# One block of 128 rows in 32 is fetched row by row by SP and ACT in place of an indirect transfer

## The chip, the cores and the metric

The kernel runs on one core of a Trainium2 chip. The metric is the device time of one execution in microseconds (us). Five engines work side by side, each from its own queue: TensorE (PE), VectorE (DVE), ScalarE (ACT), GpSimd (POOL) and SyncE (SP). They wait for each other through semaphores. SP, ACT and POOL can issue DMA transfers.

## The reference

Four graph layers over 12500 nodes of 64 features and 212500 edges (src, dst), sorted by dst. Every layer begins with h = relu(layernorm(x)), and adds its result to x:

```python
h = jnp.maximum(_layernorm(x, axis=-1), 0.0)
x = x + _L0_gnn_ref(h, edge_index, edge_attr_64, ...)   # an edge MLP on h[src], h[dst] and attributes
h = jnp.maximum(_layernorm(x, axis=-1), 0.0)
x = x + _L1_gnn_ref(h, ...)                             # messages Ht[edge_type, src], summed by dst, then a GRU cell
h = jnp.maximum(_layernorm(x, axis=-1), 0.0)
x = x + _L2_gnn_ref(h, src, dst, edge_attr_8, ...)      # pair interaction on src and dst, summed by dst
h = jnp.maximum(_layernorm(x, axis=-1), 0.0)
x = x + _L3_gnn_ref(h, edge_index, ...)                 # two SAGE convolutions, each a mean of h[src] over dst
```

In three places the work on the edges is only this: fetch one row of 64 floats per edge from a table, and sum the rows by destination.

## The kernel before

The edges are cut into 416 chunks of 512 edges, a chunk into four blocks of 128. Eight chunks (RING) make a turn, so a stage has 52 turns (ITERS). The stages over the edges, in order:

- stage 0 (e = 0): the edge MLP, without gathers of rows;
- stage 1 (e = 1): plain gather from tab_msg, which has a row per node and edge type, and the GRU cell on the nodes;
- stage 2 (e = 2): gather from tab_u and the pair interaction;
- stage 3 (e = 3): plain gather from tab_h, and the first convolution on the nodes;
- stage 4 (e = 4): plain gather from tab_q, and the last sum.

In a plain stage each engine runs its own loop over turns and chunks. For chunk u of turn it:

- DVE writes the row numbers of the chunk's 512 edges into idx (L867) and a 0/1 matrix that says which node of a window of 64 each edge belongs to (L846).
- POOL waits for idx_ready and for agg_done of the same chunk of the turn before (L659 to L661; the buffers are RING = 8 chunks deep), and issues four indirect transfers, one a block (L666). Each brings 128 rows of 256 B, one into every partition, and adds 16 to gathered[u].
- PE waits until gathered[u] has the four transfers' count, and multiplies the rows by the 0/1 matrix in four matmuls with their weight loads (L1397; the trace shows eight instructions of each kind). The last adds one to agg_done.
- DVE adds the sum to acc (L836).

Nodes are dealt with in groups of 256 (49 groups) in the same loops, one group a turn, from turn WAIT_TURNS = 5 on, since by then all edges of the first group have been summed. The chain of a group in stage 1 goes back and forth: ACT copies h and the sums (L1262, L1263), PE transposes (L1500), ACT lifts (L1284), PE multiplies (L1508, L1509), ACT applies the sigmoid (L1286), DVE mixes, ACT applies tanh (L1288), DVE updates and normalises, PE transposes (L1516), ACT lifts (L1290), PE multiplies (L1521), ACT applies tanh (L1292), PE multiplies (L1527), DVE copies, and SP stores the rows in two tables (L508). PE takes its parts at fixed places among the chunks of the turn: before chunk 1, 2, 6 and 7 and after chunk 7. Stage 3 has a chain of the same kind with four steps of ACT after its copies and one store; in stage 4 it is one copy of ACT, one transpose, one step of DVE and one store.

In the plain stages ACT and SP do nothing else. Their loops run over the groups alone:

```python
            def groups(e, chain):
                with act.Fori(0, P) as p:
                    ...
                    with act.Fori(0, min(SG, whole)) as g:
                        chain(ga, turn0, g)
```

P, the number of passes over the edges, is 1 for this input. Addresses that are known only at run time go through registers: SP and DVE load the eight window starts of a turn in one instruction (L347), and a transfer or an operation then takes its address from a register.

## Time and profile before

| what | value |
|---|---|
| median of 3 runs | 10297.66 us (10293.77 to 10303.55) |
| the profiled execution | 10296.52 us, span 10294.9 us |
| busy: PE, DVE, ACT, POOL | 5755.4, 4349.8, 2458.5, 6906.9 us |
| mean granted TensorE clock | 0.687 of full speed |
| gathers (L666) | 4 x 1664, of 944 ns each (median) |
| first and last gather: stage 1, 2 | 1774.3 to 3855.9 us, 3907.6 to 6019.5 us |
| first and last gather: stage 3, 4 | 6088.1 to 8169.1 us, 8206.0 to 10281.9 us |

The span runs from the first to the last instruction of the program. Busy counts an engine's work, not its sequencer: register operations, semaphores, branches and the issue of transfers from SP and ACT are not counted as busy. PEq, SPq and the like are the sequencers.

### The profile page before, as it was taken

Reading aid. Unit: us, or ns where it says so; the run is one execution under the profiler, and the core shown is the slowest. Engines: PE = TensorE matmul, PEld = TensorE weight load, DVE = VectorE, ACT = ScalarE, POOL = GpSimd, SP = SyncE. Lnnn points to the kernel's source line nnn. Section 1 sums busy time; section 2 is a strip of 40 time slices with the busy share of each in tenths; the row PEclk is TensorE's granted clock in tenths of the full one; section 3 lists DMA queues with packets and bytes.
Section 4 is the critical chain, followed back from the end, with each engine's and each line's share of the span. In section 5 each row is a group of like instructions: output and inputs, shape, how many; then the busy total and the mean of one; then the engine's idle time right before and its main releaser. Section 6 shows DMA issues by size and latency. Waiting matters only on the chain.

```text
span 10294.9 us, 143864 instructions
## 1 busy us (share of the span) xinstructions
PE 5755.4 (56%) x32026; PEld 3571.8 (35%) x32026; DVE 4349.8 (42%) x12092; ACT 2458.5 (24%) x4667; POOL 6906.9 (67%) x7939
## 2 busy tenths in 40 slices
PE   6999996244444447999999963333333322222222
PEld 4777774222222223444444422322222211111111
DVE  6888885123232225777777751111111111111111
ACT  5999994000000002333333310000000000000000
POOL 3333332777777776777777757777777677777777
PEclk9999998555555558999999975555555555555555
DMA  3333333111111112222222211111111111111111
GB/s 105 97 96 96 97 96 123 27 30 29 30 29 30 29 29 53 61 61 62 61 60 61 61 35 27 28 28 28 28 28 28 24 27 28 28 28 28 28 28 27
DMA packets 503896, 488.63 MB, mean 47 GB/s; under 512 B 245340, under 2 KB 299425, under 8 KB 503777
## 3 DMA queue, kind: packets, MB, share of 16 engines
q0 software_dynamic: 220480, 235.58, 12.0%
q1 hardware_dynamic: 283360, 252.43, 8.5%
q8 instruction: 20, 0.33, 0.0%
q14 instruction: 36, 0.29, 0.0%
HBM read 427.04 MB, written 61.15 MB: 47 GB/s over the span
## 4 chain that ended last, share of the span: by engine, by line
POOL 46%; PE 27%; issue 18%; DVE 5%; POOLq 1%; ACT 1%; DVEq 1%; DMA 0%; SPq 0%; ACTq 0%
POOL mov L666 44%; PE ps L1563 6%; PE ps L1423 4%; PE ps L1397 3%; PE ps L1555 3%; PE ps L1430 3%; POOL outs L666 1%; PE ps L1582 1%; DVE scr L936 1%; PE ps L1548 1%; PE ps L1544 1%; PE ps L1573 1%; PE ps L1421 1%; PE ps L1477 1%; PE ps L1437 1%
## 5 line engine op out<-in xcount | busy, mean ns | idle before, releaser
L1397 PE MATMUL ps<-outs,mov 128*64 128x64 f32 x9984 | 1371.1, 319 | 4213.4 <-DMA mov<-tab_q,idx 1507.2
L1397 PEld LDWEIGHTS ps<-outs,mov 128*64 128x64 f32 x9984 | 1158.7, 222 | 4541.2 <-issue 4541.2
L836 DVE TENSOR_TENSOR acc<-acc,ps 64x64 f32 (+1 forms) x1664 | 353.8, 213 | 4428.8 <-PE ps L1397 4426.9
L666 POOL DMA_INDIRECT outs<-tab_u,idx x1664 | 1584.0, 952 | 579.6 <-issue 478.1
L666 POOL DMA_INDIRECT mov<-tab_h,idx x1664 | 1575.1, 947 | 574.5 <-issue 506.5
L666 POOL DMA_INDIRECT mov<-tab_q,idx x1664 | 1570.0, 944 | 542.8 <-issue 506.5
L666 POOL DMA_INDIRECT mov<-tab_msg,idx x1664 | 1575.8, 947 | 532.6 <-issue 491.9
L936 DVE TENSOR_TENSOR scr<-ps,scr 128x512 f32<-128x512 f32 x1664 | 1064.2, 686 | 363.4 <-PE ps L1555 336.5
L1563 PE MATMUL ps<-scr,w_bas 128*64 128x512 f32 x3328 | 899.0, 618 | 0.0
L632 POOL TENSOR_TENSOR scr<-outs 128x128 f32<-128x128 f32 x416 | 192.0, 462 | 813.3 <-DVE outs L846 812.5
L846 DVE TENSOR_TENSOR outs<-rel,iota_w 128x256 f32<-128x256 f32 x1664 | 706.3, 425 | 43.2 <-issue 29.8
L1319 ACT ACTIVATE scr<-ps 64x512 f32<-64x512 f32 x832 | 492.3, 592 | 496.9 <-PE ps L1548 465.7
L1555 PE MATMUL ps<-bas,pair 128*128 128x512 bf16 x1664 | 528.5, 386 | 100.5 <-DVE scr L936 100.5
L1263 ACT ACTIVATE scr<-acc 64x256 f32 (+3 forms) x196 | 79.9, 408 | 2087.7 <-DVE acc L836 2075.5
L1423 PE MATMUL ps<-w_l0m,scr 128*128 128x128 f32 x3328 | 481.9, 288 | 0.0
L1430 PE MATMUL ps<-mov,win 128*128 128x512 f32 x832 | 449.7, 622 | 16.8 <-DVE mov L856 15.4
L1397 PE MATMUL ps<-outs,scr 128*128 128x64 f32 x3328 | 439.5, 275 | 0.0
L1423 PEld LDWEIGHTS ps<-w_l0m,scr 128*128 128x128 f32 x3328 | 402.6, 191 | 95.0 <-issue 95.0
L1397 PEld LDWEIGHTS ps<-outs,scr 128*128 128x128 f32 x3328 | 405.0, 192 | 0.0
L894 DVE SCALAR_TENSOR_TENSOR scr<-ps,scr 128x512 f32<-128x512 f32 x416 | 287.8, 692 | 182.3 <-ACT scr L1230 169.4
L1555 PEld LDWEIGHTS ps<-bas,pair 128*128 128x128 bf16 x1664 | 161.2, 97 | 537.6 <-DVE scr L936 491.8
L1262 ACT ACTIVATE scr<-h_nodes 128x128 f32 (+1 forms) x98 | 30.4, 310 | 1319.1 <-DVE acc L836 1319.1
(230 smaller groups left out, 8429.3 us busy)
## 6 DMA issues: line engine op xcount, KB each, us to landing
mov<-in_dst_row SPq DMA_DIRECT2D x832, 128.0 KB, 2.6
mov<-in_ea_T SPq DMA_DIRECT2D x416, 128.0 KB, 2.5
tab_msg<-outs SPq DMA_DIRECT2D x104, 256.0 KB, 2.0
mov<-tab_msg,idx POOLq DMA_INDIRECT x1664
outs<-tab_u,idx POOLq DMA_INDIRECT x1664
mov<-tab_h,idx POOLq DMA_INDIRECT x1664
mov<-tab_q,idx POOLq DMA_INDIRECT x1664
win<-tab_g SPq DMA_DIRECT2D x416, 32.0 KB, 2.4
```

Of the source, the lines that this page charges most:

```text
L632: nc.gpsimd.tensor_tensor(sel_half[:, u % 2], sel(0, u)[:, 0:2, :], sel(0, u)[:, 2:4, :], ALU.add) \
L666: nc.gpsimd.indirect_dma_start(out=gat(e, u)[:, k, :], out_offset=None, in_=table, in_offset=bass.IndirectOffsetOnAxis(ap=idx[:, u, k:k + ...
L836: nc.vector.tensor_tensor(into, into, bank(banks[u % len(banks)])[0:rows, 0:W], ALU.add) \
L846: nc.vector.tensor_tensor(sel(e, u), at_.unsqueeze(2).to_broadcast([P128, TL, W]), iota_w[:, :].unsqueeze(1).to_broadcast([P128, TL, W]), ...
L894: nc.vector.scalar_tensor_tensor(out=hid1[:, u % 2, :], in0=bank(u % 2), scalar=0.0, in1=soft1[:, u % 2, :], op0=ALU.max, op1=ALU.add) \
L936: nc.vector.tensor_tensor(zed[:, b % SL, :], bank(2 + b % 2), inter[:, u % 2, b % 2, :], ALU.mult) \
L1319: ins = nc.scalar.activation(inter[h_ * D:(h_ + 1) * D, u % 2, s, :], bank(u % 2)[s * D:(s + 1) * D, :], ACT.Copy)
L1397: last = mm(bank(banks[u % len(banks)])[0:width, 0:W], values(u)[:, k, :], sel(e, u)[:, k, :], start=k == 0, stop=k == TL - 1)
L1423: last = mm(out_[:, k, :], hid1[:, u % 2, k * P128:(k + 1) * P128], w_l0m[:, :], start=False, stop=k == TL - 1)
L1430: mm(bank(u % 2), win[:, u % SL, :], mov[:, u % SL, :], start=True, stop=True).then_inc(mm1_done, 1)
L1555: mm(bank(2 + b % 2), pair[:, b, :], bas[:, u, :], start=True, stop=True).then_inc(bas_spread, 1)
L1563: mm(bank(4)[(b % 2) * D:(b % 2 + 1) * D, :], w_bas[:, b // 2, :], zed[:, b % SL, :], start=b < 2, stop=b >= NBAS - 2).then_inc(weighed, 1)
```

## The change

In stages 1, 3 and 4, block 3 of chunk 7 of every turn (FETCHED) is no longer gathered by POOL. SP fetches its rows 0 to 63 and ACT its rows 64 to 127, each row with a transfer of its own of 256 B from table[row number] to one partition.

Per turn, SP and ACT each:

- wait for the list of row numbers of the turn (64 integers in one partition, in a part of w_l0m or w_l0n that is free by then; a transfer per turn, issued one turn ahead, from src_em or from row_numbers_em, a new copy of row_i in HBM);
- load the numbers into registers in eight parts of eight (FR), the first part before they wait for agg_done of chunk 7 of the turn before, whose buffer the rows go to;
- issue eight transfers per part; ahead of the last part's they issue the list of the next turn.

SP's stores of a group move into this loop, after part 3 (counted from 0), one turn later than the group's chain. ACT's chain of a group and the eight parts share one sequence, in the order that the diff shows. PE waits, for chunk 7, for three gathers and for both engines' 64 rows.

```diff
+FETCHED = (RING - 1, TL - 1)
+SP_ROWS = 64
+FR = 8
+ACT_ROWS = P128 - SP_ROWS
...
+        row_numbers_em = dram("row_numbers_em", [P128, CH * TL], I32)
...
+        FETCH = {1: 0, 3: 1, 4: 2}
...
+        def fetched_here(e, u, k):
+
+            return e in FETCH and (u, k) == FETCHED
+
+        def gathered_by(P, e, p, it, u):
+
+            per = {n: sum(not fetched_here(n, u, k) for k in range(TL)) for n in GATHER}
+            whole = sum(per[n] for n in GATHER if GATHER[n] < GATHER[e])
+            return P * (16 * ITERS * whole) + p * (16 * ITERS * per[e]) + it * (16 * per[e]) + 16 * per[e]
+
+        def list_rows(eng, e, it, first, count, to, listed):
+
+            u, k = FETCHED
+            numbers = row_numbers_em if e == 1 else t["src_em"]
+            col = it * (RING * TL) + (u * TL + k)
+            eng.dma_start(to, numbers[first:first + count, bass.ds(col, 1)].rearrange("p a -> a p"), allow_slow_non_contiguous=True)                .then_inc(listed, 16)
+
+        def row_numbers(kind, e, numbers, part):
+
+            return nc.values_load_multi_w_load_instructions(
+                numbers[:, part * FR:(part + 1) * FR], engines=[kind], min_val=0, max_val=(NP * NT if e == 1 else NP) - 1,
+                skip_runtime_bounds_check_because="the lists hold numbers of nodes and of edge types")[1]
+
+        def fetch_rows(eng, e, table, first, part, rows, rows_in):
+
+            u, k = FETCHED
+            for n in range(FR):
+                at_ = first + part * FR + n
+                eng.dma_start(gat(e, u)[at_:at_ + 1, k, :], table[bass.ds(rows[n], 1), :]).then_inc(rows_in, 16)
...
+            sp.dma_start(row_numbers_em, row_i[:, :]).then_inc(rows_kept, 16)
...
-            def store_flow(flow, tables):
+            def fetch_and_store(e, table, flow, tables, behind):
+
                 with sp.Fori(0, P) as p:
                     turn0 = sp.snap(p * SG)
-                    with sp.Fori(0, SG) as g:
-                        store_rows(flow, g, turn0, tables, lambda g: rows_out)
-
-            store_flow(gru_of, [tab_u, tab_v])
+                    ga = sp.snap((P * e + p) * CH)
+
+                    listed = sp.snap((P * FETCH[e] + p) * ITERS)
+
+                    def turn(it, with_store, last=False):
+                        sp.wait_ge(sp_listed, (listed + it) * 16 + 16)
+                        sp.sem_inc(sp_turn, 1)
+                        for part in range(SP_ROWS // FR):
+                            rows = row_numbers(mybir.EngineType.SP, e, sp_list, part)
+                            if part == 0:
+                                sp.wait_ge(agg_done, done(ga, it, FETCHED[0], RING))
+                                sp.sem_inc(sp_turn, 1)
+                            if part == SP_ROWS // FR - 1 and not last:
+                                list_rows(sp, e, it + 1, 0, SP_ROWS, sp_list, sp_listed)
+                            fetch_rows(sp, e, table, 0, part, rows, sp_fetched)
+                            if with_store and part == 3:
+                                store_rows(flow, it - behind, turn0, tables, lambda g: rows_out)
+
+                    list_rows(sp, e, 0, 0, SP_ROWS, sp_list, sp_listed)
+                    with sp.Fori(0, behind) as it:
+                        turn(it, False)
+                    with sp.Fori(behind, ITERS - 1) as it:
+                        turn(it, True)
+                    turn(ITERS - 1, True, True)
+                    for n in range(ITERS - behind, SG):
+                        store_rows(flow, n, turn0, tables, lambda g: rows_out)
+
+            wait_stores(sp, None)
+            sp.wait_ge(rows_kept, 16)
+            fetch_and_store(1, tab_msg, gru_of, [tab_u, tab_v], WAIT_TURNS + 1)
...
-            store_flow(conv_of, [tab_q])
-            store_flow(out_of, [out])
+            wait_flow_end(sp, sp_turn, sum_of, P)
+            fetch_and_store(3, tab_h, conv_of, [tab_q], WAIT_TURNS + 1)
+            wait_flow_end(sp, sp_turn, conv_of, P)
+            fetch_and_store(4, tab_q, out_of, [out], WAIT_TURNS)
...
                         for k in range(TL):
+                            if fetched_here(e, u, k):
+                                continue
...
-            def groups(e, chain):
+            def fetch_and_groups(e, table, chain):
                 with act.Fori(0, P) as p:
                     ga = sums_whole(e, p)
                     turn0 = act.snap(p * SG)
-                    whole = ITERS - WAIT_TURNS + 1
-                    with act.Fori(0, min(SG, whole)) as g:
-                        chain(ga, turn0, g)
-                    for g in range(whole, SG):
-                        chain(ga, turn0, g)
-
-            def gru_chain(ga, turn0, g):
+
+                    listed = act.snap((P * FETCH[e] + p) * ITERS)
+
+                    def rows_of(it, last=False):
+
+                        def rows(part):
+                            if part == 0:
+                                act.wait_ge(act_listed, (listed + it) * 16 + 16)
+                                act.sem_inc(act_turn, 1)
+                            rows_ = row_numbers(mybir.EngineType.Activation, e, act_list, part)
+                            if part == 0:
+                                act.wait_ge(agg_done, done(ga, it, FETCHED[0], RING))
+                                act.sem_inc(act_turn, 1)
+                            if part == ACT_ROWS // FR - 1 and not last:
+                                list_rows(act, e, it + 1, SP_ROWS, ACT_ROWS, act_list, act_listed)
+                            fetch_rows(act, e, table, SP_ROWS, part, rows_, act_fetched)
+                        return rows
+
+                    list_rows(act, e, 0, SP_ROWS, ACT_ROWS, act_list, act_listed)
+                    with act.Fori(0, WAIT_TURNS) as it:
+                        rows = rows_of(it)
+                        for part in range(ACT_ROWS // FR):
+                            rows(part)
+                    with act.Fori(WAIT_TURNS, ITERS - 1) as it:
+                        chain(ga, turn0, it - WAIT_TURNS, rows_of(it))
+                    chain(ga, turn0, ITERS - 1 - WAIT_TURNS, rows_of(ITERS - 1, True))
+                    for g in range(ITERS - WAIT_TURNS, SG):
+                        chain(ga, turn0, g, lambda part: None)
+
+            def gru_chain(ga, turn0, g, rows):
                 f = gru_of
+                rows(0)
                 take_sums(f, ga, turn0, g, D, own_sum, True)
                 wait_flow(act, f, "turned", turn0, g)
                 nc.scalar.activation(hT[0:D, 0, 0:SN], bank(0)[0:D, 0:SN], ACT.Copy).then_inc(f.sems["lifted"], 1)
+                rows(1)
                 wait_flow(act, f, "formed", turn0, g)
                 nc.scalar.activation(gates, by_block(bank(1))[:, :, 0:2 * D], ACT.Sigmoid).then_inc(f.sems["shaped"], 1)
+                rows(2)
                 wait_flow(act, f, "mixed", turn0, g, 1)
                 nc.scalar.activation(cand, cand, ACT.Tanh).then_inc(f.sems["shaped"], 1)
+                rows(3)
+                rows(4)
+                rows(5)
                 wait_flow(act, f, "turned", turn0, g, 1)
                 nc.scalar.activation(hT[0:D, 1, 0:SN], bank(2)[0:D, 0:SN], ACT.Copy).then_inc(f.sems["lifted"], 1)
+                rows(6)
                 wait_flow(act, f, "formed", turn0, g, 1)
                 nc.scalar.activation(tT[0:D, 0, 0:SN], bank(3)[0:D, 0:SN], ACT.Tanh).then_inc(f.sems["shaped"], 1)
-
...
+            fetch_and_groups(1, tab_msg, gru_chain)
...
-            groups(3, conv_chain)
-
-            def out_chain(ga, turn0, g):
+            wait_flow_end(act, act_turn, sum_of, P)
+            fetch_and_groups(3, tab_h, conv_chain)
+
+            def out_chain(ga, turn0, g, rows):
+                rows(0)
                 take_sums(out_of, ga, turn0, g, D, own_sum, False)
+                for part in range(1, 5):
+                    rows(part)
                 taken(out_of, "settled", turn0, g)
-
-            groups(4, out_chain)
+                for part in range(5, ACT_ROWS // FR):
+                    rows(part)
+
+            wait_flow_end(act, act_turn, conv_of, P)
+            fetch_and_groups(4, tab_q, out_chain)
 
 
         @block.tensor
...
             def gathered_here(e, p):
-                gg = pe.snap((P * GATHER[e] + p) * ITERS)
-                return lambda it, u: pe.wait_ge(gathered[u], (gg + it) * (16 * TL) + 16 * TL)
+                fetched = pe.snap((P * FETCH[e] + p) * ITERS) if e in FETCH else None
+
+                def here(it, u):
+                    pe.wait_ge(gathered[u], gathered_by(P, e, p, it, u))
+                    if e in FETCH and u == FETCHED[0]:
+                        pe.sem_inc(pe_turn, 1)
+                        pe.wait_ge(sp_fetched, (fetched + it) * (16 * SP_ROWS) + 16 * SP_ROWS)
+                        pe.sem_inc(pe_turn, 1)
+                        pe.wait_ge(act_fetched, (fetched + it) * (16 * ACT_ROWS) + 16 * ACT_ROWS)
+                        pe.sem_inc(pe_turn, 1)
+                return here
```

## Rows read from the trace of the kernel before

**Rows 1.** The page: POOL's busy time, and the chain that ended last.
```profile
...
POOL 46%; PE 27%; issue 18%; DVE 5%; POOLq 1%; ACT 1%; DVEq 1%; DMA 0%; SPq 0%; ACTq 0%
POOL mov L666 44%; PE ps L1563 6%; PE ps L1423 4%; PE ps L1397 3%; PE ps L1555 3%; PE ps L1430 3%; POOL outs L666 1%; PE ps L1582 1%; DVE scr L936 1%; PE ps L1548 1%; PE ps L1544 1%; PE ps L1573 1%; PE ps L1421 1%; PE ps L1477 1%; PE ps L1437 1%
```

**Rows 2.** Windows of stages 1, 3 and 4; columns as in the first line.
```profile
core 0: us, PE busy (x) PEld busy (x) DVE busy (x) ACT busy (x) POOL busy (x), PEclk, DMA share, GB/s
1780.00:3858.00 2078.00, 815.51 (x4162) 549.11 (x4162) 575.94 (x2406) 114.89 (x329) 1571.26 (x1660) 0.50 0.15 29
6096.00:8172.00 2076.00, 782.65 (x4252) 594.24 (x4252) 374.54 (x1467) 102.38 (x282) 1569.04 (x1658) 0.50 0.15 28
8214.00:10285.00 2071.00, 473.69 (x3406) 397.82 (x3406) 345.65 (x1372) 19.57 (x47) 1563.81 (x1658) 0.50 0.15 28
```

**Rows 3.** Waits in stage 1: engine, awaited, us in total, times, longest.
```profile
ACT hT L1290 <- PE ps L1516: 492.8, 37, 13.9
POOL mov L666 <- issue: 353.5, 1160, 0.3
```

**Rows 4.** Timeline of POOL in stage 1, then the gather's line (duration min/median/max).
```profile
3739.53 0.94 POOL L666 DMA_INDIRECT mov<-tab_msg,idx  x1 [0.30 <-issue]
3740.78 0.94 POOL L666 DMA_INDIRECT mov<-tab_msg,idx  x1 [0.30 <-issue]
...
L666 POOL DMA_INDIRECT mov<-tab_msg,idx x1664: 940/944/1213, 1774.3 to 3855.9; - x185
```

**Rows 5.** SP's timeline before stage 0: issues of one-row transfers.
```profile
32.41 0.44 SPq L438 DMA_DIRECT2D w_pp<-in_pp_b  x1
32.89 0.25 SPq L438 DMA_DIRECT2D w_ii<-in_ii_b  x1
...
54.04 0.83 SPq L449 DMA_DIRECT2D bias_parts<-outs  x3
55.70 0.23 SPq L451 DMA_DIRECT2D bpart<-bias_parts  x1
```

**Rows 6.** SP's timeline in stage 2: issues with addresses from registers.
```profile
3909.68 0.49 SPq L537 DMA_DIRECT2D mov<-in_dst_row  x1
3910.35 0.47 SPq L540 DMA_DIRECT2D win<-tab_v  x1
3911.01 0.41 SPq L542 DMA_DIRECT2D bas<-basis_parts  x1
```

**Rows 7.** Loads of eight registers: two of stage 0, then two of stage 2.
```profile
L347 SPq TENSOR_LOAD <-base_i x47: 521/527/531, 209.7 to 1491.9; - x47
L347 DVEq TENSOR_LOAD <-base_i x47: 594/597/601, 217.6 to 1499.8; - x47
...
L347 DVEq TENSOR_LOAD <-base_i x44: 1841/1846/1862, 4126.9 to 5893.7; - x44
L347 SPq TENSOR_LOAD <-base_i x44: 694/699/705, 4130.8 to 5897.7; - x44
```

**Rows 8.** SP's stores in stage 1: issue in ns, and landing.
```profile
L508 SPq DMA_DIRECT2D tab_v<-scr x38: 420/420/427, 2099.7 to 3582.0; - x38
...
L508 SPq DMA_DIRECT2D tab_u<-scr x37: 377/377/378, 2139.4 to 3581.6; - x37
...
DMA to landing us min/median/max: 1.7/1.9/2.1
```

**Rows 9.** Timelines: ACT at stage 1's end, PE's eight matmuls of a chunk within it.
```profile
3862.11 0.31 ACT L1262 ACTIVATE scr<-h_nodes 128x128 f32 x1 [6.24 <-DVE acc L836]
...
3863.51 0.38 ACT L1284 ACTIVATE hT<-ps 64x256 f32<-64x256 f32 x1 [0.79 <-PE ps L1500]
3868.64 0.38 ACT L1286 ACTIVATE scr<-ps 128x256 f32<-128x256 f32 x1 [4.76 <-PE ps L1509]
...
3743.57 1.11 PE L1397 MATMUL ps<-outs,mov 128*64 128x64 f32 x8 [2.90 <-DMA mov<-tab_msg,idx]
```

More of the change, by code:

```diff
@@ L179, in build_gnn @@
         r_pib2 = raw[0:1, 8 * D:9 * D]
+        sp_list = w_l0m[0:1, 0:SP_ROWS].bitcast(I32)
+        act_list = w_l0n[0:1, 0:ACT_ROWS].bitcast(I32)
         r_b, r_bd = raw[0:1, 9 * D:11 * D], raw[0:1, 12 * D:14 * D]
@@ L246, in build_gnn @@
         settled = sem("settled")
+        rows_kept = sem("rows_kept")
+        sp_listed = sem("sp_listed")
+        act_listed = sem("act_listed")
+        sp_fetched = sem("sp_fetched")
+        act_fetched = sem("act_fetched")
         stored = [sem(f"stored{n}") for n in range(GB)]
@@ L1284, in gru_chain, with conv_chain @@
                 nc.scalar.activation(hT[0:D, 0, 0:SN], bank(0)[0:D, 0:SN], ACT.Copy).then_inc(f.sems["lifted"], 1)
+                rows(1)
                 wait_flow(act, f, "formed", turn0, g)
                 nc.scalar.activation(gates, by_block(bank(1))[:, :, 0:2 * D], ACT.Sigmoid).then_inc(f.sems["shaped"], 1)
+                rows(2)
                 wait_flow(act, f, "mixed", turn0, g, 1)
                 nc.scalar.activation(cand, cand, ACT.Tanh).then_inc(f.sems["shaped"], 1)
+                rows(3)
+                rows(4)
+                rows(5)
                 wait_flow(act, f, "turned", turn0, g, 1)
                 nc.scalar.activation(hT[0:D, 1, 0:SN], bank(2)[0:D, 0:SN], ACT.Copy).then_inc(f.sems["lifted"], 1)
+                rows(6)
                 wait_flow(act, f, "formed", turn0, g, 1)
                 nc.scalar.activation(tT[0:D, 0, 0:SN], bank(3)[0:D, 0:SN], ACT.Tanh).then_inc(f.sems["shaped"], 1)
-            def conv_chain(ga, turn0, g):
+                rows(7)
+            def conv_chain(ga, turn0, g, rows):
                 f = conv_of
+                rows(0)
                 take_sums(f, ga, turn0, g, D, own_sum, True)
@@ L1298, in conv_chain @@
                 nc.scalar.activation(hT[0:D, 0, 0:SN], bank(0)[0:D, 0:SN], ACT.Copy).then_inc(f.sems["lifted"], 1)
+                rows(1)
                 wait_flow(act, f, "formed", turn0, g)
@@ L1301, in conv_chain @@
                     .then_inc(f.sems["shaped"], 1)
+                rows(2)
                 wait_flow(act, f, "mixed", turn0, g)
                 nc.scalar.activation(hidn, hidn, ACT.Relu).then_inc(f.sems["shaped"], 1)
+                rows(3)
+                rows(4)
+                rows(5)
                 wait_flow(act, f, "turned", turn0, g, 1)
                 nc.scalar.activation(tT[:, 0, 0:SN], bank(2)[:, 0:SN], ACT.Copy).then_inc(f.sems["lifted"], 1)
-            groups(1, gru_chain)
+                rows(6)
+                rows(7)
+            wait_stores(act, None)
+            act.wait_ge(rows_kept, 16)
+            fetch_and_groups(1, tab_msg, gru_chain)
             act.preload_act_table_set("exp_and_others")
@@ L1337, in _ @@
                                                    (3, lambda g: taken(sum_of, "ordered", turn0, g))]))
-            groups(3, conv_chain)
-            def out_chain(ga, turn0, g):
+            wait_flow_end(act, act_turn, sum_of, P)
+            fetch_and_groups(3, tab_h, conv_chain)
+            def out_chain(ga, turn0, g, rows):
+                rows(0)
                 take_sums(out_of, ga, turn0, g, D, own_sum, False)
+                for part in range(1, 5):
+                    rows(part)
                 taken(out_of, "settled", turn0, g)
-            groups(4, out_chain)
+                for part in range(5, ACT_ROWS // FR):
+                    rows(part)
+            wait_flow_end(act, act_turn, conv_of, P)
+            fetch_and_groups(4, tab_q, out_chain)
         @block.tensor
```

## Prediction

> **What bounds the kernel now.** I read the page first. POOL is busy 67% of the span and its gather line alone makes up 44% of the chain that ended last [rows 1]. The windows per stage come next [rows 2]: in the three plain gather stages (1, 3 and 4) POOL is busy 1560 to 1570 us of some 2075, PE at most 816, DVE 576, ACT 115. The missing quarter of POOL is no wait on anyone: its longest wait in stage 1 is "issue", 1160 times at most 0.3 us [rows 3], and the timeline shows a gather of 0.94 us started every 1.25 us without a break [rows 4]. The 1664 gathers of stage 1 start between 1774.3 and 3855.9: 2081.6/1663 = 1.252 us each. So a turn of 8 chunks, 32 gathers, lasts 32 x 1.252 = 40.06 us (SP's 37 stores between 2139.4 and 3581.6 give 1442.2/36 = 40.06 too [rows 8]), and 52 turns make each of the three stages. TensorE is granted half its speed there (0.50 in the clock column, 1.2 GHz) and is idle for most of it. SP and ACT have room: SP issues two stores a turn, ACT spends most of a turn waiting, 492.8 us in 37 turns for one transpose [rows 3]. Stage 2 keeps all its gathers, so it stays.
>
> **What is taken away.** One gather in 32, in three stages: 1.252 x 52 x 3 = 195.3 us. A turn bound by POOL then takes 31 x 1.252 = 38.81 us. Whether it comes to that depends on two rings that the change creates. Block 3 of chunk 7 has one buffer. SP and ACT may fill it only once PE has used it (agg_done of the turn before), and PE can take chunk 7 only when 64 rows of each have landed. So a turn is the longest of POOL's 38.81, SP's ring and ACT's ring. POOL itself is not held up by a late chunk 7: its buffers are 8 chunks deep, a turn's worth.
>
> **Price of a row.** No row fetch with an address from a register is in the trace. The nearest: SP's issue of one 256 or 512 B row takes 0.23 to 0.25 us behind another small one (three in 0.83 us, with the gaps), and 0.44 right behind a 64-row transfer [rows 5]. Between an issue and the next one that needs a new address lie 0.18 to 0.19 us (3909.68 + 0.49 to 3910.35; 3910.35 + 0.47 to 3911.01) [rows 6]. Behind a row stands a row, so I take 0.25 + 0.19 = 0.44 us, 28.2 for 64. Low end 0.23 + 0.18 = 0.41 (26.2); high end 0.44 + 0.19 = 0.63 (40.3).
>
> **The other terms of a ring.** Eight registers are loaded per 8 rows. On SP such a load takes 0.53 us without gathers beside it and 0.70 with them, on DVE 1.85 with them [rows 7]. The first of a turn comes ahead of the wait on the buffer and is covered; seven at 0.70 + 0.04 of dispatch are 5.2 us. On ACT the load isn't shown; I take SP's 0.70, with 0.53 and 1.85 as ends. The list of the next turn is one 64-element transfer: 0.47 issue like the 64-row one of [rows 6], 0.14 for its address, 0.19 because the small issue behind it lasts 0.44 in place of 0.25: 0.8. Its landing is covered by the eight rows behind it (3.5 us) and what follows. The last row's landing: 1.09 us from issue to a released waiter for one row [rows 5], 1.7 to 2.1 for the 256-row stores [rows 8]; I take 1.8 from the issue's start, 1.55 from its end (ends 0.85 and 1.85). PE's eight instructions of chunk 7 take 1.11 us [rows 9], with 0.2 for two handovers 1.3; entry 0.1. Bare ring: 28.2 + 5.2 + 0.8 + 1.55 + 1.3 + 0.1 = 37.15 us.
>
> The Trainium skill bears on the open load price (SBUF — State Buffer, Terms): DVE and GpSimd share a pair of ports that one holds exclusively, while ACT has its own. By that ACT would load like SP, not like DVE; the rows show DVE's slowdown beside gathers (0.60 to 1.85) but nothing of ACT's. If it is wrong, the sum is the rival on loads below.
>
> **SP's ring.** Its stores stand inside: two in stage 1, 0.38 + 0.42 [rows 8] + 0.14 + 0.09 addresses + 0.19 for the small issue behind, 1.2 us; one in stages 3 and 4, 0.75. That is 38.4 and 37.9 us: both under 38.81, by 0.4 and 0.9 only. The stored group was settled a turn earlier, so its wait costs nothing.
>
> **ACT's ring.** Here the chain of node steps stands in the same queue. An activation runs while the sequencer goes on, so I count dispatch, 0.15 each, and those waits that rows don't cover. The end of stage 1, where no gather holds PE up, gives them [rows 9]: from the first copy to the lift 1.40 us (3862.11 to 3863.51), from the lift to the gates 5.13 (3863.51 to 3868.64).
> - Stage 4: one copy, one wait long met: 37.15 + 0.4 = 37.6, hidden under POOL.
> - Stage 3: 1.40 + 0.15 until the lift, four more steps 0.6, each behind 4.3 us of rows that cover it: 39.3.
> - Stage 1: 1.55; then the gates need 5.13 plus the part of chunk 1 (1.11) that the lift doesn't cover, 0.7, against 4.3 of rows: 1.5 of waiting; five more steps 0.75: 41.0. The later waits (13 us today [rows 3]) lie behind three parts of rows, 12.9 us.
>
> **The sum.** Five turns of a stage have no chain and run at 38.81. Stage 1: 5 x 38.81 + 47 x 41.0 = 2121, against 52 x 40.06 = 2083: +38. Stage 3: 194 + 47 x 39.3 = 2041: -42. Stage 4: 52 x 38.81 = 2018: -65. A last chunk that waits for rows, and the waits on the flows' ends before a stage, 3 us a stage: +9. The copy of the row numbers to HBM, 832 KB, is one more issue of some 0.4 us ahead of stage 0; even uncovered it is nothing beside the rest. Total -60: 10296.5 - 60 = 10237 us. The profiled execution (10296.52, span 10294.9) is 1.1 us under the median of 10297.66, which is nothing beside this.
>
> 0.01 us on a row is 0.64 us a turn, 0.64 x 94 = 60 us in stages 1 and 3 and up to 33 more in stage 4; the forecast stands on thin margins.
>
> **Rivals.**
> 1. *The rings are shorter than POOL's turn everywhere.* Rows at 0.41 take 2.0 us off and loads at 0.53 another 1.2: ACT's ring in stage 1, with 0.4 more of waiting for the gates, is 38.3. Then the whole saving comes: 10296.5 - 195 + 9 = 10110. For it: both prices are in the trace. Against: SP's load was 0.70 when gathers ran beside. 0.17.
> 2. *The rings eat the saving.* 0.4 to 0.9 us more a turn in stages 1 and 3 than in the sum ((10277 - 10237)/94, (10318 - 10237)/94) ends within 0.2% (21 us, about what a measurement of this kernel tells from no change): 0.13.
> 3. *ACT's ring is longer and the kernel slower.* Place: ACT's queue in stages 1 and 3. Price: if issues wait until the activation ahead has ended, 0.31 + 0.40 + 4 x 0.38 = 2.2 us a turn in two stages, 2.2 x 94 = +207: 10444. Or rows of 0.48: +2.6 on the ring, 94 x 2.6 + 52 x 1.4 in stage 4 + 10 x 0.9 in the turns without a chain = +326: 10560. It decides from 0.9 us a turn on, and reaches 10700 with rows near 0.49 to 0.50. Middle 10450. For it: no ACT issue is shown, every term was taken bare; against: the ACT records follow each other without a drain. 0.23.
> 4. *ACT loads registers as DVE does*, 1.85: 7 x 1.15 = 8.0 us a turn, rings 49.0, 47.3 and 45.6: 47 x 8.9 + 47 x 7.2 + 52 x 5.5 + 10 x 5.1 = +1094, with the 9 above: 11400. Or each row issue is stretched to 0.63 by the one before: +12.1 a turn, rings 53.1, 51.4, 49.7, in the same way +1740: 12045. 0.12 together.
> 5. *Rows follow each other only after landing.* One row per 1.09 us is 70 us, some 80 a turn: 10296.5 + 40 x 156 = 16500. Against: three rows issued from 54.04 on had all landed when the waiter went on at 55.70 [rows 5]; in line they would have needed 3.3 us, to 57.3. 0.05, with whatever else goes past 10700. The Trainium skill (DMA: Bandwidth & Descriptors, Why a DMA increments its semaphore by 16 and not by 1) has such a row on one engine, the lowest-numbered, so all 128 of a turn would meet there; no row of this profile tells the engine of a one-row transfer.
>
> **Chances and range.** The case of the sum, 10150 to 10277, has 0.27; the rivals in their order 0.17, 0.13, 0.23, 0.12 and 0.05; 0.03 is left for slower in a way not named. Faster by over 0.2%: 0.27 + 0.17 = 0.44; same 0.13; slower 0.23 + 0.12 + 0.05 + 0.03 = 0.43. The range 10105 to 10700 holds the sum's case and rivals 1 to 3, 0.80. The likeliest case's own range is 10150 to 10277.
>
> **What the profile after would show.** POOL's spacing stays 1.25 us. If the sum is right, stage 4 takes about 2018 us with POOL without idle time; in stage 1 POOL waits about 2 us a turn on PE, and PE waits for the rows, not for a gather, ahead of chunk 7. SP's and ACT's row issues stand 0.44 us apart; ACT's load rows are 0.5 to 0.7. What makes it wrong: an issue over 0.47 or a load near 1.85 on ACT, an activation that holds up the issue behind it, rows that land later than 2 us, or a loop body of over 200 instructions that has to be fetched anew each turn (the packets of the instruction queues would rise far over the few that they are now).

## The result, and the profile after

| | before | after |
|---|---|---|
| median, us | 10296.93 (10293.77 to 10303.55, 4 runs) | 10131.76 (10130.24 to 10133.27, 4 runs) |
| profiled span, us | 10294.9 | 10128.6 |
| gathers, stage 1 | 1774.3 to 3855.9 | 1778.7 to 3807.7 |
| gathers, stage 3 | 6088.1 to 8169.1 | 6039.9 to 8060.4 |
| gathers, stage 4 | 8206.0 to 10281.9 | 8097.7 to 10115.5 |

The ratio is 0.9838, 95% interval 0.9826 to 0.985: 165 us less, where 60 less was forecast. From first to last gather, stages 1, 3 and 4 are 52.6, 60.4 and 58.1 us shorter, 171.1 in all. The rest of the span is 4.8 us longer, 4.4 of them ahead of the first gather of stage 1. That start was 1778.0 in a kernel without the fetches and 1774.2 in one with them (below), so I don't lay it to the fetches; its cause stays open. The span is the time from the first to the last instruction of the profiled execution; the medians are of all runs.

First the windows of the three stages after, with the columns of [rows 2]:

```profile
core 0: us, PE busy (x) PEld busy (x) DVE busy (x) ACT busy (x) POOL busy (x), PEclk, DMA share, GB/s
1783.00:3808.00 2025.00, 810.79 (x4162) 549.16 (x4162) 577.67 (x2406) 114.25 (x328) 1534.09 (x1609) 0.50 0.17 30
6044.00:8061.00 2017.00, 784.50 (x4260) 598.58 (x4260) 374.82 (x1467) 102.20 (x282) 1526.05 (x1610) 0.50 0.16 29
8102.00:10116.00 2014.00, 474.62 (x3414) 398.57 (x3414) 346.51 (x1373) 19.57 (x47) 1523.14 (x1609) 0.50 0.16 29
```

PE, DVE and ACT do the work of [rows 2] within the same busy time; POOL has 37 to 43 us less. The granted clock is 0.50 as before (1.2 GHz). Whether POOL still sets the pace is a matter of its waits. In stage 1 from 2100 to 3600, which answers to [rows 3]:

```profile
PE ps L1520 <- DMA mov<-tab_msg,idx: 546.9, 153, 4.3
ACT hT L1394 <- PE ps L1648: 450.7, 38, 12.0
POOL mov L741 <- issue: 340.2, 1114, 0.3
PE ps L1520 <- DMA mov<-tab_msg: 234.6, 38, 6.5
...
POOL mov L741 <- DVE idx L942: 23.8, 78, 0.3
```

POOL's longest wait is 0.3 us, its ordinary gap. It never waits on PE. Over the whole of the three stages the gaps between its gathers are 305 ns on average, as before; the one pause over 0.4 us is 1.6 us between the first two gathers of stage 3. PE does wait for the fetched rows (the entry without idx), 38 times and up to 6.5 us, but what that holds up, chunk 7's release, POOL needs only a turn later. From 6400 to 7900, in stage 3, it is 38 times and up to 4.8 us; from 8500 to 10000, in stage 4, the list of waits has none.

The new work, from the timelines of ACT and of SP over about one turn of stage 1:

```profile
3027.78 0.55 ACTq L379 DMA_DIRECT2D w_l0n<-row_numbers_em  x1
3028.50 8.89 ACTq L392 DMA_DIRECT2D mov<-tab_msg  x16
3037.74 0.31 ACT L1337 ACTIVATE scr<-h_nodes 128x128 f32 x1 [10.49 <-issue]
3037.96 0.40 ACT L1338 ACTIVATE scr<-acc 64x256 f32 x1
3039.15 0.38 ACT L1383 ACTIVATE hT<-ps 64x256 f32<-64x256 f32 x1 [0.79 <-PE ps L1632]
3040.04 3.14 ACTq L392 DMA_DIRECT2D mov<-tab_msg  x8
3044.79 0.38 ACT L1386 ACTIVATE scr<-ps 128x256 f32<-128x256 f32 x1 [5.27 <-PE ps L1641]
3045.68 3.03 ACTq L392 DMA_DIRECT2D mov<-tab_msg  x8
3048.82 0.31 ACT L1389 ACTIVATE scr<-scr 128x128 f32<-128x128 f32 x1 [3.65 <-issue]
3049.72 11.14 ACTq L392 DMA_DIRECT2D mov<-tab_msg  x24
3060.91 0.38 ACT L1394 ACTIVATE hT<-ps 64x256 f32<-64x256 f32 x1 [11.78 <-PE ps L1648]
```

```profile
3026.74 23.09 SPq L392 DMA_DIRECT2D mov<-tab_msg  x40
3050.37 0.42 SPq L552 DMA_DIRECT2D tab_u<-scr  x1
3050.89 0.42 SPq L552 DMA_DIRECT2D tab_v<-scr  x1
3052.40 11.50 SPq L392 DMA_DIRECT2D mov<-tab_msg  x24
3064.99 0.56 SPq L379 DMA_DIRECT2D w_l0m<-row_numbers_em  x1
3065.74 3.20 SPq L392 DMA_DIRECT2D mov<-tab_msg  x8
```

A merged line holds the register loads that stand between its rows. On ACT 24 rows with two loads take 11.14 us and 8 rows 3.03 to 3.18, so a part of eight rows with its load is (11.14 - 3.10)/2 = 4.02 us; on SP it is (11.50 - 3.20)/2 = 4.15. The instructions' own times, by line, from 3000 to 3600:

```profile
L392 SPq DMA_DIRECT2D mov<-tab_msg x984: 224/228/360, 2999.9 to 3599.7; - x197
L392 ACTq DMA_DIRECT2D mov<-tab_msg x984: 213/213/593, 3001.0 to 3599.8; - x197
...
L383 ACTq TENSOR_LOAD <-w_l0n x123: 715/724/867, 3000.1 to 3596.2; - x123
L383 SPq TENSOR_LOAD <-w_l0m x123: 682/784/928, 3002.6 to 3598.7; - x123
```

PE takes chunk 7 of this turn when ACT's last row, whose issue ends at 3067.51 + 3.18 = 3070.69, has landed:

```profile
3072.12 1.09 PE L1520 MATMUL ps<-outs,mov 128*64 128x64 f32 x8 [6.28 <-DMA mov<-tab_msg]
```

### The profile page after: what moved, and what is told of

Same layout as the page of the kernel before. It is cut to its first block, busy times and chain, and to the rows that moved or that the text cites. A ratio compares the mean times of both kernels' runs of the same rounds, so it can differ in the third digit from the quotient of the medians.

```text
span 10128.6 us, 209066 instructions
## 1 busy us (share of the span) xinstructions
PE 5756.1 (57%) x32026; PEld 3578.1 (35%) x32026; DVE 4352.4 (43%) x12092; ACT 2451.7 (24%) x4667; POOL 6779.5 (67%) x7783
## 4 chain that ended last, share of the span: by engine, by line
POOL 35%; PE 32%; issue 16%; DVE 7%; ACTq 5%; DMA 3%; ACT 1%; POOLq 1%; DVEq 1%; SPq 0%
POOL mov L741 33%; PE ps L1695 6%; PE ps L1520 5%; PE ps L1546 4%; ACTq L392 4%; PE ps L1553 3%; PE ps L1687 3%; POOL outs L741 2%; PE ps L1714 1%; DVE scr L1011 1%; PE ps L1680 1%; PE ps L1676 1%; PE ps L1544 1%; DMA mov<-tab_msg,idx 1%; PE ps L1705 1%
## 5 line engine op out<-in xcount | busy, mean ns | idle before, releaser
L741 POOL DMA_INDIRECT mov<-tab_h,idx x1612 | 1528.7, 948 | 559.6 <-issue 469.6
L741 POOL DMA_INDIRECT mov<-tab_msg,idx x1612 | 1538.1, 954 | 518.2 <-issue 463.2
L741 POOL DMA_INDIRECT mov<-tab_q,idx x1612 | 1527.0, 947 | 528.1 <-issue 490.9
L921 DVE TENSOR_TENSOR outs<-rel,iota_w 128x256 f32<-128x256 f32 x1664 | 706.2, 425 | 42.4 <-issue 29.0
```

The lines of the kernel that those rows point to most:

```text
L741: nc.gpsimd.indirect_dma_start(out=gat(e, u)[:, k, :], out_offset=None, in_=table, in_offset=bass.IndirectOffsetOnAxis(ap=idx[:, u, k:k + ...
L921: nc.vector.tensor_tensor(sel(e, u), at_.unsqueeze(2).to_broadcast([P128, TL, W]), iota_w[:, :].unsqueeze(1).to_broadcast([P128, TL, W]), ...
```

## The experiments

Before them stood three theories. **A**: all three rings are shorter than POOL's turn, POOL paces every stage (the forecast's rival 1), and less than 195 us comes because gathers became longer. **B**: ACT's ring paces stages 1 and 3, as forecast, only less so. **C**, beside either: the traffic of the rows stretches POOL's gathers. Behind the first four runs came **D**: what stretches them is where they fall against DVE's operations. The turns below are those of the list's issue, (last start - first start)/(n - 1), unless a row says otherwise.

### The block left out, and fetched by nobody (e1_left_out)

The kernel before, with block 3 of chunk 7 left out in stages 1, 3 and 4; PE multiplies stale rows there. Cuts inside a diff are marked with three dots, here and below.

```diff
+LEFT_OUT = (RING - 1, TL - 1)
...
+                            if left_out(e, u, k):
+                                continue
...
-                return lambda it, u: pe.wait_ge(gathered[u], (gg + it) * (16 * TL) + 16 * TL)
+                return lambda it, u: pe.wait_ge(gathered[u], gathered_by(P, e, p, it, u))
```

> The kernel before, with block 3 of chunk 7 of every turn left out in stages 1, 3 and 4: POOL issues 31 gathers, SP and ACT keep their old loops, and nobody fetches the 128 rows (the sums lack the right rows of these edges). It gives what the removal alone is worth. Theory A (POOL sets the pace of all three stages of the changed kernel, and both rings of the row fetches are shorter than its turn): the time is that of the changed kernel but for the few us of stretched gathers, 10105 to 10135. Theory B (ACT's ring sets the pace in stages 1 and 3 of the changed kernel, by 0.1 to 0.3 us a turn): 10102 to 10115, with no gather longer than before. Theory C (the row traffic stretches gathers, 1.1 us in place of 0.94): the stretched gathers, 110, 36 and 42 by stage, fall back to the 34, 18 and 1 of before; if they stay, they come from the phase between POOL and DVE and not from the rows.

Measured: 10110.56 us (10109.67 to 10112.39, 4 runs), ratio 0.9811 (0.9795 to 0.9828), span 10108.6. The removal alone is worth 195 us by the medians of that chip (10305.34 - 10110.56), where 195.3 was forecast, and 186 by the profiled spans (10294.9 - 10108.6). The two disagree because the kernel before took 10305.34 us beside this one, and 10296.93 beside the changed kernel. What the 128 row fetches of a turn cost in the whole kernel is therefore 20 us by the spans and 30 by the medians (195 against 165), and the intervals of the two ratios overlap; what follows rests on single durations in the traces. Its gathers by line, then those of the changed kernel (the numbers are: busy us, mean ns, idle before):

```profile
L677 POOL DMA_INDIRECT mov<-tab_h,idx x1612 | 1532.1, 950 | 559.4 <-issue 478.2
L677 POOL DMA_INDIRECT mov<-tab_q,idx x1612 | 1521.2, 944 | 526.6 <-issue 490.7
L677 POOL DMA_INDIRECT mov<-tab_msg,idx x1612 | 1526.0, 947 | 517.2 <-issue 462.3
```

```profile
L741 POOL DMA_INDIRECT mov<-tab_h,idx x1612 | 1528.7, 948 | 559.6 <-issue 469.6
L741 POOL DMA_INDIRECT mov<-tab_msg,idx x1612 | 1538.1, 954 | 518.2 <-issue 463.2
L741 POOL DMA_INDIRECT mov<-tab_q,idx x1612 | 1527.0, 947 | 528.1 <-issue 490.9
```

The idle columns agree within 1.5 us: POOL waits no more with the fetches than without, which speaks against B. The gathers themselves take 12.1 us more in stage 1 and 5.8 in stage 4, and 3.4 less in stage 3: 14.5 of the 20. Most take 944 ns; those over 1000 number 110, 36 and 42 (stages 1, 3, 4) in the changed kernel, 27, 38 and 1 without the fetches, and 34, 18 and 1 in the kernel before.

### The rings by themselves (e2_rings64)

Blocks 2 and 3 of every chunk are not gathered in the plain stages, so POOL has 16 gathers (20 us) a turn; SP and ACT fetch as before. Nearly half of the rows are stale.

```diff
+        def skipped(e, u, k):
+            return e in FETCH and k >= 2
+
...
-                            if fetched_here(e, u, k):
+                            if skipped(e, u, k):
```

> The changed kernel with only blocks 0 and 1 of each chunk gathered by POOL in stages 1, 3 and 4 (16 gathers, 20 us a turn), and 64 rows each fetched by SP and ACT as before; the other blocks are left out, so that the sums lack their right rows. Now the rings of the row fetches are the longest thing in a turn and show their own length. Theory A, with the row period of 0.37 us and parts of 3.94 us as the changed kernel's trace has them: about 38.3 us a turn in stage 1, 36.7 in stage 3, 36.2 in stage 4. Theory B: 39.0, 38.9 and 38.8, as in the changed kernel. The forecast's own prices (0.44 us a row): 41.0, 39.3 and 37.9.

Measured: 9841.58 us (one run, like the next). ACT's list issues in stages 1, 3 and 4:

```profile
L382 ACTq DMA_DIRECT2D w_l0n<-row_numbers_em x40: 552/552/553, 2099.8 to 3599.5; - x40
...
L382 ACTq DMA_DIRECT2D w_l0n<-in_src_em x38: 547/547/548, 6376.0 to 7749.2; - x38
...
L382 ACTq DMA_DIRECT2D w_l0n<-in_src_em x41: 547/552/552, 8213.3 to 9679.0; - x41
```

1499.7/39 = 38.45 us in stage 1, 1373.2/37 = 37.11 in stage 3, 1465.7/40 = 36.64 in stage 4. In the first turns of stage 1, without a chain, five such issues lie between 1802.4 and 1945.4: 35.75. Such a turn is the length of the longer ring, since PE waits for both engines' rows. In stage 1 ACT's last row of a turn is issued 1.3 us behind SP's, in stage 3 0.2 us, but in stage 4 SP's comes 0.9 us behind ACT's (medians of 33 turns in the trace): 38.45 and 37.11 are ACT's ring, 36.64 is SP's. In the first turns SP's last row comes 0.3 to 0.6 us behind ACT's, so 35.75 is SP's ring as well. Over it the chain lengthens the turn by 2.7 us in stage 1 (3.85 in the forecast) and 1.4 in stage 3 (2.15); ACT's own ring grows by 0.3 to 0.6 more than that. With half of the gathers beside them, all rings are under 38.81, in stage 1 by 0.4 us only. A holds, and with the idle columns above B falls.

### The rings with half the rows (e3_rings32)

As the last, with 32 rows for each engine.

```diff
-SP_ROWS = 64
+SLOTS = [[0], [1], [], [], [], [], [2], [3]]
+SP_ROWS = 32
-ACT_ROWS = P128 - SP_ROWS
+ACT_ROWS = 32
```

> As the run with the rings alone, but with 32 rows each for SP and ACT, four parts in place of eight (ACT's in places 0, 1, 6 and 7 of its chain); 64 more rows a turn are left out. The difference of the two, divided by four, is the price of a part of eight rows in place. Theory A: 3.94 us, so 22.5 us a turn in stage 1, about 21 in stages 3 and 4, where POOL's 20 us is near. The forecast's prices: 4.26 us a part. If waits of ACT's chain that the rows covered come out now, the difference is smaller than four parts: that much of the chain was covered.

Measured: 7905.47 us; turns of 20.03 us in stage 4 (42 issues, 6967.2 to 7788.1), 23.91 in stage 3 and 31.59 in stage 1. Stage 4 had reached POOL's 16 gathers, so SP's four parts are worth at least (36.64 - 20.03)/4 = 4.15 us each. Stage 1 missed its expectation of 22.5 by 9 us: fewer rows uncovered the waits of the chain, which they had hidden. With four parts beside it the chain of nodes still makes a turn of 31.59 us; some 9 us of the rows that came off had stood in time in which ACT waited.

### 72 rows for SP, 56 for ACT (e4_sp72)

```diff
-SP_ROWS = 64
+SLOTS = [[0], [1], [2], [3], [4], [], [5], [6]]
+SP_ROWS = 72
```

> The changed kernel with 72 rows for SP and 56 for ACT: ACT's ring is one part (3.9 us) shorter, SP's one longer. Theory A: no change, 10128 to 10136, stage 1 at 39.0 us a turn. Theory B: stage 1 falls to POOL's 38.8 and stage 3 to 38.8, about 15 us less, 10117. If SP's ring with 72 rows is past 38.8 us, slower: 36.7 + 4.1 = 40.8 in stage 1 and 40.3 in stages 3 and 4 would give +240 us, 10370.

Measured: 10537.04 us (10533.99 to 10541.66, 4 runs), ratio 1.0225 (1.0208 to 1.0242): slower than before. Turns of 42.15, 41.51 and 41.62 us. One part more made SP's ring the pace (SP's last row is now issued 7 to 9 us behind ACT's), 36.64 + 4.15 plus a dearer list in stage 4, and ACT's shorter ring brought nothing, as A has it and B does not. Part of it is the list itself: 72 numbers are a 0.87 us issue on SP, and 56 one of 1.28 on ACT, where 64 are 0.55 to 0.57.

### 80 rows for ACT, 48 for SP (e5_act80)

```diff
-SP_ROWS = 64
+SLOTS = [[0], [1], [2], [3], [4], [5, 6, 7], [8], [9]]
+SP_ROWS = 48
```

> The changed kernel with ACT fetching 80 rows of the block and SP 48: ACT's ring has ten parts of eight rows in place of eight, so it becomes the pace. Theory A (rings as the runs with 64 and with 72 rows show them: a part of ACT 4.05 us, its ring about 38.5 us in stage 1, 36.8 in stage 3, 35.6 in stage 4): the turn of 32 blocks takes about 46.6 us in stage 1, 44.9 in stage 3, 43.7 in stage 4, 52 turns each, about 11,040 us in all. Theory B (the forecast's prices, ACT's ring 41.0, 39.3 and 37.6 us and 0.44 us a row with 0.74 us a load, so 4.26 us a part): 49.5, 47.8 and 46.1 us, about 11,430 us.

Measured: 11048.36 us (one run); turns of 46.48, 45.08 and 43.67 us against A's 46.6, 44.9 and 43.7 and the forecast's 49.5, 47.8 and 46.1. Two turns of ACT in its stage 4:

```profile
9035.29 0.42 ACT L1339 ACTIVATE scr<-acc 64x256 f32 x1 [43.53 <-issue]
9036.18 31.73 ACTq L393 DMA_DIRECT2D mov<-tab_q  x64
9068.95 0.55 ACTq L380 DMA_DIRECT2D w_l0n<-in_src_em  x1
9069.66 8.83 ACTq L393 DMA_DIRECT2D mov<-tab_q  x16
9078.84 0.42 ACT L1339 ACTIVATE scr<-acc 64x256 f32 x1 [43.13 <-issue]
```

The queue is nearly full of row issues with their loads: 31.73 + 0.55 + 8.83 of 43.55 us. Lists of 48 and 80 numbers take 0.55 to 0.56, as 64 do.

### DVE's two steps exchanged (e6_sel_first)

The timelines show what a stretched gather has beside it. POOL, then DVE, in stage 4 of the changed kernel:

```profile
8565.95 0.94 POOL L741 DMA_INDIRECT mov<-tab_q,idx  x1 [0.31 <-issue]
8567.19 1.12 POOL L741 DMA_INDIRECT mov<-tab_q,idx  x1 [0.30 <-issue]
8568.62 0.94 POOL L741 DMA_INDIRECT mov<-tab_q,idx  x1 [0.30 <-issue]
```

```profile
8566.95 0.17 DVE L942 TENSOR_SCALAR idx<-src_i 128x4 int32 x1
8567.08 0.43 DVE L921 TENSOR_TENSOR outs<-rel,iota_w 128x256 f32<-128x256 f32 x1
```

Of the changed kernel's 4836 gathers in the three stages, 2855 run while DVE executes nothing, and none of them takes over 961 ns, though the rows are fetched beside them too. Those that start 100 to 200 ns behind the start of DVE's 0/1 matrix (L921) are all long, 113 of 113, mean 1091 ns; those that start 300 to 700 ns behind it take 940 to 953. The later such a gather starts, the shorter it is, by as much: 1129 ns on average from 100 to 120 ns behind the matrix's start, 1052 from 180 to 200. So their ends keep one distance from DVE's end: 175 of the 197 gathers over 990 ns end 811 to 841 ns behind the end of a 0/1 matrix (406 to 427 ns long), and 18 end 813 to 820 ns behind the end of a step of the node chain (L1126, 291 to 293 ns long). They also sit at fixed places of the turn: in stage 4, 45 of 46 are the fourth gather, in stage 1, 98 of 115 the 8th, the 17th or the 21st. The exchange makes the 0/1 matrix start earlier:

```diff
-                return lambda p: [(0, idx_stage(e, p, numbers)), (1, sel_stage(e, p)),
+                return lambda p: [(1, sel_stage(e, p)), (0, idx_stage(e, p, numbers)),
```

> The changed kernel with one edit: in each chunk of a plain stage DVE makes the 0/1 matrices before the float-to-int copy of the index column, not behind it. The copy takes about 0.13 us, so the 0/1 operation should start about 0.13 us earlier against the gathers of POOL. Theory D (a gather that starts 60 to 200 ns behind the start of DVE's 0/1 operation waits for that operation's end; this, and not the row traffic, is why the changed kernel has 110, 36 and 42 stretched gathers in stages 1, 3 and 4, worth 17.2, 7.6 and 5.9 us): the offset moves out of the window at most of the fixed places, most stretched gathers go, 10 to 17 us less than the changed kernel, 10115 to 10122 us. Rival C (the row traffic of the two rings stretches them): the same number of stretched gathers, the changed kernel's 10132 us within 5. A third outcome would be that other gathers fall into the window instead: the same or a little slower, 10130 to 10145, with the stretched gathers at other places of the turn, which would still speak for D.

Measured: 10123.59 us (10119.19 to 10125.44, 5 runs), ratio 0.9828 (0.9815 to 0.9841); 1.6 us above the range that D expected. The same place of the turn in its stage 4, one turn later, DVE and then POOL:

```profile
8596.76 0.41 DVE L921 TENSOR_TENSOR outs<-rel,iota_w 128x256 f32<-128x256 f32 x1
8597.09 0.15 DVE L942 TENSOR_SCALAR idx<-src_i 128x4 int32 x1
...
8597.15 0.94 POOL L741 DMA_INDIRECT mov<-tab_q,idx  x1 [0.30 <-issue]
```

The gather now starts 390 ns behind the 0/1 matrix and takes 944. Stage 4 went from 42 long gathers to 7, stage 1 from 110 to 86 (17.2 to 9.8 us over 944), stage 3 from 36 to 46 (7.6 to 11.5), 41 of them beside both the 0/1 matrix and a step of the node chain (L1205). The rows are fetched as before, so C doesn't explain stage 4.

### The changed kernel again, and the exchange in stages 1 and 4 alone (e7_again, e8_sel_1_4)

```diff
+                def stages(p):
+                    first = [(0, idx_stage(e, p, numbers)), (1, sel_stage(e, p))]
+                    return (first if e == 3 else first[::-1]) + [(7, add_stage(e, p, D, range(4, 8)))]
+                return stages
```

> The changed kernel as it is, timed on the same chip and against the same runs of the kernel before as the run with the other order of DVE in stages 1 and 4, so that those two can be set side by side. All theories: the ratio of the first timing again, 0.984 within its interval, 110, 36 and 42 stretched gathers within a few, about 10132 us by the earlier chip.

> The changed kernel with DVE's 0/1 matrices ahead of the index copy in stages 1 and 4, and in the old order in stage 3. In the run with the new order everywhere the stretched gathers cost 9.8, 11.5 and 2.5 us in stages 1, 3 and 4, against 17.2, 7.6 and 5.9 in the old order; stage 3 got worse by a DVE operation of the node chain that came to lie ahead of a gather. Theory D (the place of DVE's wide operations against the gathers sets the stretching, stage by stage): 9.8 + 7.6 + 2.5, so 10 to 12 us less than the changed kernel of the same call, a ratio to the kernel before of about 0.9826. Rival: the 8 us seen between the two orders was only the difference between calls, and this run and the changed kernel are within 3 us of each other.

Measured on the same chip, 5 runs each: 10130.84 us (10126.33 to 10132.19) for the changed kernel, ratio 0.9837, and 10122.48 us (10113.55 to 10124.6) with the exchange, ratio 0.9827 (0.9813 to 0.984). The two ranges don't overlap; 8.4 us less, where D expected 10 to 12 and its rival under 3. Their gathers, in the same order:

```profile
L741 POOL DMA_INDIRECT mov<-tab_h,idx x1612 | 1527.9, 948 | 560.4 <-issue 468.8
L741 POOL DMA_INDIRECT mov<-tab_msg,idx x1612 | 1539.1, 955 | 517.5 <-issue 464.6
L741 POOL DMA_INDIRECT mov<-tab_q,idx x1612 | 1526.9, 947 | 528.2 <-issue 491.4
```

```profile
L741 POOL DMA_INDIRECT mov<-tab_h,idx x1612 | 1530.6, 949 | 561.7 <-issue 467.5
L741 POOL DMA_INDIRECT mov<-tab_msg,idx x1612 | 1532.2, 951 | 517.6 <-issue 455.0
L741 POOL DMA_INDIRECT mov<-tab_q,idx x1612 | 1523.9, 945 | 528.2 <-issue 444.4
```

By these lines stage 1 gains 6.9 us and stage 4 3.0; stage 3, whose code is the same, loses 2.7 (45 gathers over 1000 ns in place of 36), so a stage's share moves by some us on its own. This is the fastest version, by 0.08% over the changed kernel.

## Why the prediction was right in direction and wrong in size

**POOL as the bound, and the removal: right.** POOL waits on no one, 31 gathers make a turn, and leaving the block out is worth 186 to 195 us against 195.3.

**The step that failed is the term of the rings**, above all "ACT's ring": 41.0 us in stage 1 and 39.3 in stage 3 were both put over 38.81, and measured 38.45 and 37.11 in the run of the rings by themselves. Rival 1, given 0.17, is what happened: no ring is longer than POOL's turn. Its rows of 0.41 came true as an average, its loads of 0.53 did not. Term by term:

| term | forecast | measured |
|---|---|---|
| a row, issue to issue, us | 0.44 | 0.37 (ACT), 0.41 (SP) |
| the first row behind a load, issue to issue | 0.44 | 0.61 (ACT), 0.45 (SP) |
| a load of eight registers with its dispatch | 0.74 | 0.72 (ACT), 0.78 (SP) plus dispatch |
| a part of eight rows | 4.26 | 4.02 (ACT), 4.15 (SP) |
| the turn's list | 0.8 | 0.72 (3027.78 to 3028.50) plus its address |
| last row's issue to PE's start | 1.55 | 1.43 (3070.69 to 3072.12), with its handover |
| bare ring | 37.15 | 35.75 |
| chain on ACT, stage 1, over the bare ring | 3.85 | 2.7 |
| chain on ACT, stage 3, over the bare ring | 2.15 | 1.4 |
| SP's store, stage 4 | 0.75 | 0.9 |

- *The row.* The issue is 213 ns on ACT and 228 on SP where 250 was taken from [rows 5]; the address is 37 + 29 ns of register work plus dispatch, 0.156 in all on ACT and 0.183 on SP, where 0.19 was taken from [rows 6]. In the run of eight at 3045.68 the last seven rows stand 0.369 apart and only the first, behind the load, has an issue of 0.448: 0.213 + 7 x 0.369 + 0.235 = 3.03 us, forecast 7 x 0.44 + 0.25 = 3.33. With that first row the spacing within a part is 0.41 on average on ACT and 0.42 on SP, the low end of the forecast and not its middle. With the loads between them this is 0.24 us a part, 1.9 a ring, of which the other terms took 0.5 back: 1.4 us on the bare ring. "0.01 us on a row is 60 us" was the right warning; it cut the good way.
- *The steps of the chain.* In stage 3 the 1.4 us bring 39.3 under 38.81. In stage 1 they don't (41.0 - 1.4 = 39.6): there the chain's term failed too, by 0.8 to 1.15 us. It held 0.75 for the dispatch of five steps at 0.15 each. Where the rows cover a step's wait, the trace has 0.13 us from the end of the row ahead to the load behind (3048.71 to 3048.84), and 0.06 (3060.86 to 3060.92) where 0.03 stands without a step between.
- *The loads.* 0.72 to 0.78 with gathers beside them, as taken from SP, and nothing like DVE's 1.85. The Trainium skill (SBUF — State Buffer, Terms) has ACT on ports of its own, and DVE and GpSimd on a shared pair; ACT's load of 0.72 agrees with it.
- *The chain in ACT's queue.* No stall stood behind an activation: L1389 starts at 3048.82 and lasts 0.31 us, and the load of the next part starts at 3048.84 beside it. Rival 3's first form falls, and its second (rows of 0.48) with it.

**Stage by stage.** Forecast +38, -42, -65, and +9 for the ends; measured -52.6, -60.4, -58.1, and +4.8. With ACT's ring out of the way the forecast's own pace, 52 x 38.81 = 2018 us, would have stood for every stage: the failed term is 103 us in stage 1 (2121 to 2018) and 23 in stage 3 (2041 to 2018), against measured 2029.0 and 2020.6. In stage 4, where the forecast had POOL as the pace, 2018 met the measured 2017.8, but partly by luck: gathers spaced as in that stage before, 2075.9/1663 = 1.248 us, make 52 x 31 x 1.248 = 2012, and 6 us of longer gathers filled the rest. The gain there was 58 and not 65, since I took 2083 for every stage and stage 4 took 2075.9.

**From 195 to 165.** By the spans the gain is 166.3 us, 29.0 less than 195.3. Of these, 20.0 separate the changed kernel from the one with the block left out; 14.5 of them are the gathers' own duration, as the two lists of lines show. Of the other 9, 7 lie in stage 3 of the kernel with the block left out: it is 57.6 us shorter than before (6025.0 to 8048.4), where stage 1 is 65.6 and stage 4 64.7. Its long gathers cost 11.2 us over 944 in place of 5.4, without any row being fetched, and the pause of 1.6 us behind its first gather, which the kernel before lacks, costs 1.3. Its stage 1 also starts 3.7 us later than before. With the medians in place of the spans, all of the 30 us stand between the changed kernel and this one, and the split is not settled to better than 10 us.

**Rival 5.** Rows of one queue overlap: 64 of ACT's rows of a turn in the fifth experiment's timeline went out in 31.73 us, 0.50 a row with the loads, where one after the other would take 1.09 each, and in the changed kernel PE starts 1.43 us behind the last issue, so they had landed too. The trace of the changed kernel shows each row of ACT as one packet of 256 B and one write of 4 B to a semaphore: its queue has 9984 packets of 256 B for its 3 x 52 x 64 rows. By the Trainium skill (DMA: Bandwidth & Descriptors, Why a DMA increments its semaphore by 16 and not by 1) such a row, read as a transfer that isn't split, goes to one DMA engine, the lowest-numbered. One packet a row agrees with one engine a row; no row here tells which engine it is, and if it is the same for all, it carried them. **Rival 2**, an end within 0.2%, and **rival 4**, DVE-like loads, fall with the measured parts. The instruction queue took 65 packets in place of 36 over the whole kernel, so no loop body is fetched anew each turn.

**What stayed close.** One part of eight rows more on SP or two on ACT make the kernel 2.2% and 7.2% slower than before (10537.04/10305.34, 11048.36/10301.39). The result stands on 0.4 us a turn in stage 1 and 2.2 in stage 4, as the rings by themselves have it.

**Open.** That a gather which starts shortly behind DVE's operation ends 0.81 to 0.84 us behind that operation's end is shown; why is argued. The shared pair of ports would explain it (the Trainium skill, SBUF — State Buffer, Terms: one of DVE and GpSimd holds the pair for a whole instruction, and the other is blocked), but no run changed the ports. Nor is it shown why the changed kernel has more such gathers. PE waits for the fetched rows ahead of chunk 7, which may shift DVE's operations against the gathers; a change of the row traffic with DVE's phase held still was not tried. The 4.4 us ahead of stage 1 are open too.

## What to carry to other kernels

When work is moved into rings on idle queues, compare each ring with the bound's turn, and where the margin is under a few per cent, say so rather than add up bounds that all lean the same way: a sum of small terms, some of them rounded up, put ACT's ring on the wrong side of 38.81 in two stages. Where an engine sets the pace, what it stops doing comes back nearly in full (165 of 195 us here) as long as every other loop stays shorter, and not at all in the first one that doesn't: eight rows moved from ACT to SP decided between 1.6% faster and 2.2% slower. Waits that a long queue of small issues hides cost nothing until the issues are taken away.

## What the runs showed of the hardware

- A transfer of one row of 256 B with its address from a register costs the queue of ACT 0.37 us and that of SP 0.41, of it 213 and 228 ns for the issue; the first behind a register load costs 0.61 and 0.45. Eight rows with a load of eight registers cost 4.02 and 4.15.
- A gather of 128 rows by POOL, else 944 ns, lasts 1.04 to 1.17 us when it starts 100 to 200 ns behind the start of DVE's 128x256 operation (0.43 us), 113 times of 113, and ends 0.81 to 0.84 us behind that operation's end; one that starts 300 to 700 ns behind it takes 940 to 953 ns. DVE's operation takes 426 ns (median) beside either.
- The issue of a list of 4-byte numbers from a strided column into one partition takes 0.54 to 0.57 us (medians) for 32, 48, 64 and 80 numbers, but 0.86 to 0.87 (SP) for 72 and 1.28 (ACT) for 56.
